# One rounding moved behind a product in block 1, and six matmuls moved forward in the last down projection

## The chip, the cores and the metric

The kernel runs on one NeuronCore of a Trainium2 chip. The metric is the device time of one execution in microseconds (us). The kernel before took 323.59 us, the median of three runs (323.27, 323.59, 323.6).

## What is computed

The input x has 128 batch rows, 32 channels and 512 positions. The reference does this:

```python
y = irfft(rfft(u, 2L) * rfft(K, 2L))[..., :L] + u * D     # one long convolution per channel, K from the parameters
y = y * mask                                              # positions below a length
gate = fp8(y / s) @ gate_w.T ;  up = fp8(y / s) @ up_w.T  # 512 -> 1376
hidden = silu(gate) * up
out = x + fp8(hidden / s) @ down_w.T                      # 1376 -> 512
```

`fp8` clips to 448, rounds to float8_e4m3 and gives the value back as a wide number. The kernel builds that rounding from ordinary operations: a magnitude (ACT), a sum with the magnitude (DVE), a difference that leaves the rounded value in bf16 (DVE), and a clip (DVE).

## The kernel before, in words

The 32 channels are worked in 8 blocks of 4 (`NBLK` = 8, g counts them), so that a block has 512 tokens (4 channels x 128 batch rows). For a block g there are three kinds of work:

- **convolution** of each channel h with its Toeplitz tile (PE, L528 into `y_ps`), masked by DVE (`mask_y`, L882), scaled and its magnitude taken by ACT (`scale_y`, L378 and L379; `magnitude_y`, L386 and L389), and rounded by DVE (`sum_y` L890, `round_y` L901, `clip_y` L908) into `yq`;
- **gate and up products**: the 1376 hidden features are cut into 11 chunks (`CH` = 11) of 128, the last of 96. A chunk takes 4 matmuls into `gate_ps` and 4 into `up_ps` (L604, each double buffered). ACT makes `sil` (L415), DVE the product `hv` (`product`, L917). Chunks go in pairs (`PAIRS` = 6, the last is one chunk): ACT takes the magnitude `hc` of a pair (`abs_prod`, L397), DVE makes `ht` (`rounded_sum`, L925), rounds into `hq` (`rounded`, L934) and clips `hq` in place (`clip`, L942);
- **down projection** of the block: four row tiles t of 128 tokens, each 11 matmuls over the chunks k (`down_part`, L542), brought out by ACT (`down_scaled`, L405).

Every engine runs its own list in program order, written by hand in `slots`. Slot c of block g holds chunk c of block g, a part of the down projection of block g-1 and a part of the convolution of blocks g+1 and g+2. So when block g begins, the rounding of the last pairs of block g-1 is still to be done. On DVE that is `left_over` (L952): pairs 3, 4 and 5 of the block before, spread over slots 0, 1 and 2. It has two orders, chosen by `behind`. `behind` is true for the last block alone (L977). The ACT list of block 1 has, behind `sil` of slot 1, the magnitude of the left-over pair 5, then two magnitudes and two scalings of block 2's y, and only then `sil` of slot 2 (L408 ff.). The last block has no y work beside it.

What PE waits for: chunk n needs the products up to n-2 and `sil` up to n-2, because the banks are double buffered; the down projection of a block needs `hq_ready` for the pair of its chunk, which `clip` counts (chunks 8 and 9 are pair 4, chunk 10 is pair 5). In block 1 chunks 6 to 9 of row tile 0 are in slot 3, chunk 10 is in slot 4.

The last down projection (L645 to L660, the profile's L655) follows the last block and has no other work beside it. Row tile t has its own bank; tile 3 is computed as columns 0 to 383 and then columns 384 to 511. DVE adds the residual x to each finished tile (`residual`, L949) and SP stores it (L282); the last store ends the kernel.

Of the kernel before, what the change touches and what calls it, by code (L numbers as in the profile page):

```python
# [28 lines left out]
P = 128  # L29
# [4 lines left out]
NBLK = C // HB  # L34
TOK = HB * B
LB = L // P
CH = -(-I // P)
# [32 lines left out]
def width(c):  # L70
    return P if c < CH - 1 else TAIL
# [7 lines left out]
def adaln_ffn_kernel(nc, xT, xn, params, scales, unit, stepped, wg_d, wu_d, wd_d, out):  # L79
# [4 lines left out]
    with ExitStack() as ctx:  # L84
# [124 lines left out]
        def last_bank(t, cols):  # L209

            return gate_ps[0] if cols.start else (down_ps[0], down_ps[1], y_ps[0], y_ps[1])[t]
# [247 lines left out]
        def _(pe):  # L459
# [183 lines left out]

            full = slice(0, L)
            for t, chunks, cols in ((0, range(6), full), (1, range(6), full), (0, range(6, 8), full), (1, range(6, 8), full),  # L645
                                    (2, range(6), full), (0, range(8, CH), full), (1, range(8, CH), full),
                                    (2, range(6, CH), full), (3, range(CH), slice(0, 3 * P)),
                                    (3, range(CH), slice(3 * P, L))):
                for k in chunks:
                    w = width(k)  # L650
                    if t == 0:
                        pe.wait_ge(hq_ready, PAIRS * (NBLK - 1) + k // 2 + 1)
                    if k == 0:
                        pe.wait_ge(out_done, EMPTY + HB * (NBLK - 2) + t + 1)
                    mm = nc.tensor.matmul(last_bank(t, cols)[:, cols], hq[1][0:w, k, t * P:(t + 1) * P],  # L655
                                          wd[0:w, k, cols], start=(k == 0), stop=(k == CH - 1))
                    if k == CH - 1:
                        mm.then_inc(down_ready, 1)
# [3 lines left out]
        def _(dve):  # L662
# [214 lines left out]
            def mask_y(g, h):  # L877
                m = HB * g + h
                q = h % 2
                at_least(dve, y_ready, m + 1)  # L880
                at_least(dve, yscaled, m - 1)
                v.tensor_tensor(ym[q][:], y_ps[q][:], mask[:].rearrange("p k b -> p (k b)"),  # L882
                                ALU.mult).then_inc(ym_done, 1)

            def sum_y(g, h):

                m = HB * g + h
                q = h % 2
                at_least(dve, yscaled, m + 1)
                v.scalar_tensor_tensor(yt[q][:], yc[q][:], FLOOR, yv[q][:], ALU.max, ALU.add).then_inc(yt_done, 1)  # L890
# [4 lines left out]
            def round_y(g, par, h):  # L895

                m = HB * g + h
                q = h % 2
                at_least(dve, yt_done, m + 1)
                at_least(dve, up_ready, CH * (g - 1))  # L900
                v.scalar_tensor_tensor(yq_of(par, h), yc[q][:].rearrange("p v (k b) -> p (v k) b", k=LB), FLOOR,  # L901
                                       yt[q][:].rearrange("p v (k b) -> p (v k) b", k=LB), ALU.max, ALU.subtract,
                                       reverse1=True).then_inc(yr_done, 1)

            def clip_y(g, par, h):

                at_least(dve, yr_done, HB * g + h + 1)
                v.tensor_scalar(yq_of(par, h), yq_of(par, h), TOP, -TOP, ALU.min, ALU.max).then_inc(yq_ready, 1)  # L908

            def product(n, m, par, c):  # L910

                b, w = (par + c) % 2, width(c)
                at_least(dve, silu_done, n + 1)
                at_least(dve, up_ready, n + 1)
                if c % 2 == 0:
                    at_least(dve, t_done, m - 2)
                v.scalar_tensor_tensor(hv[c // 2 % 3][0:w, c % 2], up_ps[b][0:w, :], fac[0:w, S_UP:S_UP + 1],  # L917
                                       sil[b][0:w, :], ALU.mult, ALU.mult).then_inc(prod_done, 1)

            def rounded_sum(m, e):  # L920

                w, k = pair_rows(e)
                at_least(dve, abs_ready, m + 1)
                at_least(dve, hr_done, m - 1)
                v.scalar_tensor_tensor(ht[e % 2][0:w, 0:k], hc[e % 2][0:w, 0:k], FLOOR, hv[e % 3][0:w, 0:k],  # L925
                                       ALU.max, ALU.add).then_inc(t_done, 1)

            def rounded(m, g, par, e):

                w, k = pair_rows(e)  # L930
                at_least(dve, t_done, m + 1)
                if e == 0:
                    at_least(dve, down_ready, READ + HB * (g - 1))
                v.scalar_tensor_tensor(hq[par][0:w, 2 * e:2 * e + k, :], hc[e % 2][0:w, 0:k], FLOOR,  # L934
                                       ht[e % 2][0:w, 0:k], ALU.max, ALU.subtract, reverse1=True).then_inc(hr_done, 1)

            def clip(m, par, e):

                w, k = pair_rows(e)
                at_least(dve, hr_done, m + 1)  # L940
                part = hq[par][0:w, 2 * e:2 * e + k, :]
                v.tensor_scalar(part, part, TOP, -TOP, ALU.min, ALU.max).then_inc(hq_ready, 1)  # L942
# [31 lines left out]

            def slots(g, par, ahead, before, plan):
                first = before is None
                behind = g == NBLK - 1  # L977
                for c in range(CH):
                    n = CH * g + c
                    m = PAIRS * g + c // 2  # L980
                    if first and c == 3:
                        rounded(m - 1, g, par, 0)
                    product(n, m, par, c)
                    if c == 0 and g - 1 in SUM_BEHIND:
                        clip(PAIRS * g - 4, 1 - par, PAIRS - 4)
                        rounded_sum(PAIRS * g - 2, PAIRS - 2)
                    if c == CH - 1 and c in plan:
                        rounded(PAIRS * g + plan[c], g, par, plan[c])
                    if c % 2 == 0 and 0 < c < CH - 1:
                        rounded_sum(m - 1, c // 2 - 1)  # L990
                    if first and c == 1:
                        round_y(1, 1, 0)
                        clip_y(1, 1, 0)
                    elif ahead and c in MASK_PLAN:
                        mask_y(g + 1, MASK_PLAN[c])
                    if c < 3 and not first:
                        left_over(g, par, c, before, behind)
                    if c in plan and c < 9 and not (first and c == 3):
                        rounded(PAIRS * g + plan[c], g, par, plan[c])
                    if ahead and c in SUM_PLAN and not (first and c == 2):  # L1000
                        sum_y(g + 1, SUM_PLAN[c])
                    if c - 1 in plan:
                        clip(PAIRS * g + plan[c - 1], par, plan[c - 1])
                    if ahead and c in ROUND_PLAN and not (first and c == 4):
                        round_y(g + 1, 1 - par, ROUND_PLAN[c])
                        clip_y(g + 1, 1 - par, ROUND_PLAN[c])
                    if c == 9 and c in plan:
                        rounded(PAIRS * g + plan[c], g, par, plan[c])
                    if c == CH - 1:
                        if ahead == 2:  # L1010
                            mask_y(g + 2, 0)
                        if g not in SUM_BEHIND:
                            if PAIRS - 3 not in plan.values():
                                clip(PAIRS * g + PAIRS - 4, par, PAIRS - 4)
                            rounded_sum(m - 1, PAIRS - 2)
# [38 lines left out]
            sum_y(1, 0)  # L1054
            dve.wait_ge(k_ready, 2 * len(K_GROUPS))
            slots(0, 0, 2, None, H_BEHIND)
            for stored_k in k_stored:
                dve.wait_ge(stored_k, 16)
            slots(1, 1, 2, H_BEHIND, H_BEHIND)
            slots(2, 0, 2, H_BEHIND, H_EVEN)  # L1060
            for g in range(3, NBLK - 2):
                slots(g, g % 2, 2, H_EVEN, H_EVEN)
# [28 lines left out]
SUM_BEHIND = (0, NBLK - 2)  # L1091
# [63 lines left out]
```

## Time and profile before

| what | value |
|---|---|
| median of three runs | 323.59 us |
| the profiled execution's own time | 324.86 us |
| its span | 323.2 us |
| PE, matmuls busy | 310.3 us (96%) |
| DVE busy | 303.1 us (94%) |
| ACT busy | 206.5 us (64%) |
| granted TensorE clock over the span | 1.0 |

The span is the time from the first to the last instruction of the profiled execution; the execution's own time is 1.66 us longer. A matmul's record is longer than its share of a stream of matmuls: neighbours overlap. The same holds for DVE's and ACT's records, so steps are read from one start to the next. PEld is the weight load of a matmul.

### The profile page before, as it was taken

The numbers are of one execution on the slowest core, as the hardware profiler recorded it, in microseconds if no ns is written. First come the engines' busy times: TensorE is split into PE (matmuls) and PEld (weight loads), VectorE is DVE, ScalarE is ACT, GpSimd is POOL, SyncE is SP. The second block draws the span as 40 slices with busy tenths as digits, with TensorE's granted clock in tenths as the row PEclk, the third lists the DMA queues.
The fourth block names the chain that finished last, engine by engine and source line by source line (L and its number), as shares of the span: only waits on it lengthen the run. The fifth ranks groups of instructions, "written<-read, shape, count | busy, mean of one in ns | idle before, by whom it ended". The sixth has DMA issues, their size and how long they took to land.

```text
span 323.2 us, 4716 instructions
## 1 busy us (share of the span) xinstructions
PE 310.3 (96%) x1591; PEld 161.8 (50%) x1591; DVE 303.1 (94%) x460; ACT 206.5 (64%) x318; POOL 13.7 (4%) x25
## 2 busy tenths in 40 slices
PE   1979999999999999999999999999999999999996
PEld 1456655545455454555455454555545554444443
DVE  6969999999999999999989999899998999999894
ACT  4938788278765868376863958366864859545550
POOL 3031000000001000010001000010000000010010
PEclk9999999999999999999999999999999999999999
DMA  6869999500001690067401690046600770070028
GB/s 201 170 174 218 240 292 363 220 1 2 0 0 13 128 357 26 1 117 243 159 0 16 126 360 19 0 80 202 239 0 0 132 261 0 3 130 0 0 26 235
DMA packets 14015, 38.42 MB, mean 119 GB/s; under 512 B 1470, under 2 KB 6558, under 8 KB 11052
## 3 DMA queue, kind: packets, MB, share of 16 engines
q1 hardware_dynamic: 8412, 26.61, 23.9%
q0 software_dynamic: 5584, 11.57, 20.5%
q8 instruction: 10, 0.16, 0.2%
q14 instruction: 9, 0.07, 0.1%
HBM read 33.93 MB, written 15.81 MB: 154 GB/s over the span
## 4 chain that ended last, share of the span: by engine, by line
PE 77%; DVE 15%; issue 3%; DMA 3%; ACT 2%; DVEq 0%; SPq 0%
PE gate_ps L604 20%; PE up_ps L604 20%; PE down_ps L542 17%; PE y_ps L528 15%; DVE hv L917 3%; DVE yq L901 2%; DVE ht L925 2%; DVE yt L890 2%; DVE hq L934 2%; PE down_ps L558 2%; PE y_ps L558 1%; DMA toep<-kpad_scratch 1%; DVE ym L882 1%; PE y_ps L655 1%; DMA kpad_scratch<-hq 1%
## 5 line engine op out<-in xcount | busy, mean ns | idle before, releaser
L415 ACT ACTIVATE sil<-gate_ps,fac 128x512 f32<-128x512 f32 (+1 forms) x88 | 59.8, 681 | 71.4 <-PE gate_ps L604 70.5
L604 PE MATMUL gate_ps<-yq,wg 128*128 128x512 bf16 (+2 forms) x372 | 89.5, 363 | 0.5 <-DVE hv L917 0.3
L604 PE MATMUL up_ps<-yq,wu 128*128 128x512 bf16 (+2 forms) x372 | 89.5, 363 | 0.0
L528 PE MATMUL y_ps<-xt,toep 128*128 128x512 f32 (+1 forms) x248 | 78.1, 434 | 0.0
L917 DVE SCALAR_TENSOR_TENSOR hv<-up_ps,fac,sil 128x512 f32<-128x512 f32 (+1 forms) x88 | 65.5, 744 | 6.9 <-ACT sil L415 3.5
L542 PE MATMUL down_ps<-wd,hq 128*128 128x512 bf16 (+1 forms) x264 | 67.9, 379 | 0.0
L397 ACT ACTIVATE hc<-hv 128x1024 f32<-128x1024 f32 (+1 forms) x48 | 47.0, 980 | 17.1 <-DVE hq L934 16.7
L604 PEld LDWEIGHTS gate_ps<-yq,wg 128*128 128x128 bf16 x372 | 36.0, 100 | 41.0 <-issue 2.2
L528 PEld LDWEIGHTS y_ps<-xt,toep 128*128 128x128 f32 x248 | 45.8, 190 | 20.0 <-issue 2.4
L604 PEld LDWEIGHTS up_ps<-yq,wu 128*128 128x128 bf16 x372 | 36.3, 100 | 38.3
L925 DVE SCALAR_TENSOR_TENSOR ht<-hc,hv 128x1024 f32<-128x1024 f32 (+1 forms) x48 | 54.2, 1129 | 0.9 <-ACT hc L397 0.9
L934 DVE SCALAR_TENSOR_TENSOR hq<-hc,ht 128x1024 bf16<-128x1024 f32 (+1 forms) x48 | 53.9, 1126 | 0.3
L542 PEld LDWEIGHTS down_ps<-wd,hq 128*128 128x128 bf16 (+1 forms) x264 | 25.8, 98 | 32.7 <-issue 12.0
L901 DVE SCALAR_TENSOR_TENSOR yq<-yc,yt 128x1024 bf16<-128x1024 f32 x32 | 39.0, 1219 | 0.4
L890 DVE SCALAR_TENSOR_TENSOR yt<-yc,yv 128x1024 f32<-128x1024 f32 x31 | 37.7, 1216 | 0.0
L386 ACT ACTIVATE yc<-ym,fac 128x512 f32<-128x512 f32 x32 | 22.9, 715 | 3.4 <-DVE yq L901 3.0
L378 ACT ACTIVATE yv<-ym,fac 128x512 f32<-128x512 f32 x31 | 22.1, 712 | 3.4 <-DVE ym L882 3.4
L389 ACT ACTIVATE yc<-ym,fac 128x512 f32<-128x512 f32 x32 | 22.8, 713 | 0.0
L379 ACT ACTIVATE yv<-ym,fac 128x512 f32<-128x512 f32 x31 | 22.0, 709 | 0.0
L882 DVE TENSOR_TENSOR ym<-y_ps,mask 128x512 f32<-128x512 f32 x31 | 21.1, 680 | 0.2 <-PE y_ps L528 0.2
L942 DVE TENSOR_SCALAR hq<-hq 128x1024 bf16<-128x1024 bf16 (+1 forms) x48 | 18.5, 396 | 0.3
L405 ACT ACTIVATE res<-down_ps,fac 128x512 f32<-128x512 f32 x26 | 17.6, 677 | 1.0 <-PE down_ps L542 1.0
(163 smaller groups left out, 133.8 us busy)
## 6 DMA issues: line engine op xcount, KB each, us to landing
xt<-in_xT SPq DMA_DIRECT2D x8, 1024.0 KB, 7.8
out<-in_x SPq DMA_DIRECT2D x7, 1024.0 KB, 5.7
out<-res POOLq DMA_DIRECT2D x7, 1024.0 KB, 7.7
toep<-kpad_scratch SPq DMA_DIRECT2D x6, 1024.0 KB, 10.1
toep<-kpad_scratch SPq DMA_DIRECT2D x8, 256.0 KB, 5.1
wd<-in_down POOLq DMA_DIRECT2D x1, 1280.0 KB, 21.9
xt<-in_x SPq DMA_DIRECT2D x1, 1024.0 KB, 7.4
out<-xt SPq DMA_DIRECT2D x3, 256.0 KB, 3.2
```

What stands on the lines that cost most here:

```text
L386: gate = nc.scalar.activation(yc[q][:, 0, :], ym[q][:], ACT.Abs, scale=fac[:, R_GATE:R_GATE + 1])
L397: nc.scalar.activation(hc[e % 2][0:w, 0:k], hv[e % 3][0:w, 0:k], ACT.Abs, scale=UP20).then_inc(abs_ready, 1)
L415: nc.scalar.activation(sil[b][0:w, :], gate_ps[b][0:w, :], ACT.Silu, scale=fac[0:w, S_GATE:S_GATE + 1]).then_inc(silu_done, 1)
L528: last = nc.tensor.matmul(y_ps[h % 2][:, d * P:L], toep[par][:, h, d * P:(d + 1) * P], xt[par][:, h, 0:L - d * P], start=(d == 0), stop=(d ...
L542: mm = nc.tensor.matmul(down_ps[t % 2][:], hq[par][0:w, k, t * P:(t + 1) * P], wd[0:w, k, :], start=(k == 0), stop=(k == CH - 1))
L604: mm = nc.tensor.matmul(ps[b][0:w, cols], wt[:, k, c * P:c * P + w], yq[par][:, version, k, cols], start=(k == 0), stop=(k == LB - 1))
L882: v.tensor_tensor(ym[q][:], y_ps[q][:], mask[:].rearrange("p k b -> p (k b)"), ALU.mult).then_inc(ym_done, 1)
L890: v.scalar_tensor_tensor(yt[q][:], yc[q][:], FLOOR, yv[q][:], ALU.max, ALU.add).then_inc(yt_done, 1)
L901: v.scalar_tensor_tensor(yq_of(par, h), yc[q][:].rearrange("p v (k b) -> p (v k) b", k=LB), FLOOR, yt[q][:].rearrange("p v (k b) -> p (v k ...
L917: v.scalar_tensor_tensor(hv[c // 2 % 3][0:w, c % 2], up_ps[b][0:w, :], fac[0:w, S_UP:S_UP + 1], sil[b][0:w, :], ALU.mult, ALU.mult).then_i ...
L925: v.scalar_tensor_tensor(ht[e % 2][0:w, 0:k], hc[e % 2][0:w, 0:k], FLOOR, hv[e % 3][0:w, 0:k], ALU.max, ALU.add).then_inc(t_done, 1)
L934: v.scalar_tensor_tensor(hq[par][0:w, 2 * e:2 * e + k, :], hc[e % 2][0:w, 0:k], FLOOR, ht[e % 2][0:w, 0:k], ALU.max, ALU.subtract, reverse ...
```

## The change

Two edits. On DVE, `left_over` takes its `behind` order in block 1 as well as in the last block (block 1 is the one whose block before, 0, is in `SUM_BEHIND` = (0, 6)). With it, in block 1, the rounding of block 0's pair 4 stands behind block 1's second product instead of ahead of it, and the clip of pair 4 with the rounding and the clip of pair 5 stands in slot 2 behind the third product and the first sum of block 1, instead of in slot 1. In the last down projection the chunks 0 to 5 of row tile 3 (columns 0 to 383) are issued ahead of chunks 8 to 10 of row tile 0.

```diff
-                                    (2, range(6), full), (0, range(8, CH), full), (1, range(8, CH), full),
-                                    (2, range(6, CH), full), (3, range(CH), slice(0, 3 * P)),
+                                    (2, range(6), full), (3, range(6), slice(0, 3 * P)),
+                                    (0, range(8, CH), full), (1, range(8, CH), full),
+                                    (2, range(6, CH), full), (3, range(6, CH), slice(0, 3 * P)),
                                     (3, range(CH), slice(3 * P, L))):
...
             def slots(g, par, ahead, before, plan):
                 first = before is None
-                behind = g == NBLK - 1
+                behind = g - 1 in SUM_BEHIND
```

DVE's order in slots 0 to 2 of block 1, where s, r and c are sum, rounding and clip of a pair and a stroke marks block 1's own pair:

```
before: product 0, c2, s4, mask, r3, r4 | product 1, c3, c4, s5, r5, c5 | product 2, s0', sum_y
after:  product 0, c2, s4, mask, r3     | product 1, c3, r4, s5         | product 2, s0', c4, r5, c5, sum_y
```

## Rows read from the trace of the kernel before

**Rows 1.** Stretches: length, busy us of PE, PEld, DVE, ACT, POOL, clock, DMA, GB/s.
```profile
75.20:85.60 10.40, 10.36 (x47) 4.87 (x45) 10.37 (x14) 7.21 (x11) 0.00 (x0) 1.00 0.01 2
...
100.00:285.00 185.00, 185.00 (x870) 95.77 (x868) 178.44 (x227) 124.25 (x188) 5.21 (x6) 1.00 0.39 109
```

**Rows 2.** The chain of waits, 72 to 86 us: start, us, what.
```profile
72.44 1.02 PE gate_ps L604 x4
...
75.62 0.86 PE down_ps L542 x4
...
85.56 0.09 issue
```

**Rows 3.** DVE in order of time, 69 to 85 us: start, us, engine, line, operation.
```profile
69.29 2.35 DVE L934 SCALAR_TENSOR_TENSOR hq<-hc,ht 128x1024 bf16<-128x1024 f32 x2
71.56 0.74 DVE L917 SCALAR_TENSOR_TENSOR hv<-up_ps,fac,sil 128x512 f32<-128x512 f32 x1
72.22 0.75 DVE L942 TENSOR_SCALAR hq<-hq 128x1024 bf16<-128x1024 bf16 x2
72.89 0.68 DVE L925 SCALAR_TENSOR_TENSOR ht<-hc,hv 96x512 f32<-96x512 f32 x1
73.60 0.69 DVE L934 SCALAR_TENSOR_TENSOR hq<-hc,ht 96x512 bf16<-96x512 f32 x1
74.32 0.29 DVE L942 TENSOR_SCALAR hq<-hq 96x512 bf16<-96x512 bf16 x1
74.53 0.74 DVE L917 SCALAR_TENSOR_TENSOR hv<-up_ps,fac,sil 128x512 f32<-128x512 f32 x1
75.23 1.23 DVE L925 SCALAR_TENSOR_TENSOR ht<-hc,hv 128x1024 f32<-128x1024 f32 x1
76.37 1.22 DVE L890 SCALAR_TENSOR_TENSOR yt<-yc,yv 128x1024 f32<-128x1024 f32 x1
...
83.16 1.22 DVE L901 SCALAR_TENSOR_TENSOR yq<-yc,yt 128x1024 bf16<-128x1024 f32 x1
84.41 0.43 DVE L908 TENSOR_SCALAR yq<-yq 128x1024 bf16<-128x1024 bf16 x1
84.75 0.75 DVE L917 SCALAR_TENSOR_TENSOR hv<-up_ps,fac,sil 128x512 f32<-128x512 f32 x1
```

**Rows 4.** ACT in order of time, 70 to 75 us, idle time before in brackets.
```profile
70.59 0.63 ACT L397 ACTIVATE hc<-hv 96x512 f32<-96x512 f32 x1 [1.61 <-DVE hq L934]
...
73.58 0.67 ACT L415 ACTIVATE sil<-gate_ps,fac 128x512 f32<-128x512 f32 x1
74.15 1.04 ACT L397 ACTIVATE hc<-hv 128x1024 f32<-128x1024 f32 x1
```

**Rows 5.** PE in order of time, slot 2 of block 1.
```profile
71.16 1.03 PE L542 MATMUL down_ps<-wd,hq 128*128 128x512 bf16 x4
```

**Rows 6.** The last block's slots 1 and 2, in order of time.
```profile
290.65 1.06 ACT L397 ACTIVATE hc<-hv 128x1024 f32<-128x1024 f32 x1 [0.93 <-DVE hq L934]
...
291.74 1.23 DVE L925 SCALAR_TENSOR_TENSOR ht<-hc,hv 128x1024 f32<-128x1024 f32 x1
```

**Rows 7.** Busy time by stretch, 18 to 22 us, columns as in rows 1.
```profile
18.00:22.00 4.00, 2.87 (x14) 2.42 (x15) 1.59 (x5) 0.91 (x2) 0.63 (x1) 1.00 0.52 186
```

**Rows 8.** The last down projection in order of time.
```profile
315.17 0.59 PE L655 MATMUL down_ps<-wd,hq 128*128 128x512 bf16 x2
315.73 0.29 DVE L942 TENSOR_SCALAR hq<-hq 96x512 bf16<-96x512 bf16 x1
316.08 1.04 PE L655 MATMUL down_ps<-wd,hq 96*128 96x512 bf16 x4 [0.32 <-DVE hq L942]
...
320.03 0.62 DVE L949 SCALAR_TENSOR_TENSOR xt<-y_ps,fac,xt 128x384 f32<-128x384 f32 x1 [1.04 <-PE y_ps L655]
```

**Rows 9.** The chain of waits at the end.
```profile
317.12 2.89 PE y_ps L655 x16
```

**Rows 10.** Busy time by stretch at the end, columns as in rows 1.
```profile
321.00:321.50 0.50, 0.00 (x0) 0.00 (x0) 0.00 (x1) 0.00 (x0) 0.00 (x0) 1.00 0.55 209
```

## The prediction, written before the run

> **What bounds the kernel now.** I read the chain of waits first, then the busy time by stretch, then the engines in order of time around both edits. The windows say where which of the two sets the pace: from 100 to 285 us PE is busy 185.00 of 185 us [rows 1], so nothing that PE loses before 100 us is ever won back; whatever delay it has at that point arrives whole at the end. From 75.2 to 85.6 us both are full: PE 10.36 and DVE 10.37 of 10.40 us [rows 1]. The chain tells how the two meet there: it leaves DVE for PE at 72.44, where the matmuls of block 1's chunk 3 begin behind product 1, and has one more crack at 85.56, an issue piece of 0.09 us ahead of chunk 7 [rows 2], whose matmuls start at 85.64. Chunk 7 needs product 5, which starts at 84.75 and takes 0.75 us [rows 3], so it is done at 85.50: chunk 7 too starts as soon as DVE lets it. Between the two DVE has no gap. The reader is to see that DVE's list from 69.29 to 85.50 is one unbroken chain that ends in a PE start, and that PE cannot catch up behind it.
>
> In the tail PE waits between the second matmul of 315.17 and the matmul of 316.08, for the clip of the last pair, 315.73 to 316.02 [rows 8].
>
> **Part 1, what it takes away.** The two roundings of 69.29 take 2.27 us to the start of product 1 (71.56 - 69.29), 1.13 each [rows 3]. With one of them gone from in front, product 1 starts at 70.42 instead of 71.56 and ends near 71.2. Chunk 3 then finds its bank free, and PE is held only by its own stream. Its four matmuls before were issued at one per 0.216 us (0.86 for four [rows 2]); from the down matmuls ahead of chunk 3, which start at 71.16 [rows 5], that gives 72.02 instead of 72.44. So 0.42 us of a PE stall goes.
>
> **Part 1, what it adds.** DVE's new order is product 1, clip 3, rounding 4, sum 5, product 2. From 70.42: product 0.66 (71.56 to 72.22), clip 0.33 (two in 0.67), rounding 1.13, sum 0.71 (72.89 to 73.60) [rows 3]; DVE would be ready for product 2 at 73.25. But product 2 needs `sil` of slot 2, and that is ACT's: ACT starts the magnitude of pair 5 at 70.59, released by rounding 3, which does not move, and works through without a bracket until `sil` of 73.58, done at 74.25 [rows 4]. Nothing in that row of seven ACT operations waits for anything that the change moves earlier. So DVE idles from 73.25 to 74.28 (74.25 and 0.03 for the semaphore). Product 2 takes 0.67 to 74.95. Next is sum 0 of block 1, which needs the magnitude that ACT runs from 74.15 to 75.19 [rows 4]: it starts at 75.22, against 75.23 before [rows 3]. DVE has idled 1.03 + 0.27 = 1.30 us, and sum 0 is where it was.
>
> Before, that time was filled: clip 4, rounding 5 and clip 5 stood ahead of product 2. Now they stand behind sum 0. Their steps are 0.33, 0.72 (73.60 to 74.32) and 0.21 (74.32 to 74.53), together 1.26 us [rows 3]. So `sum_y` starts at 77.62 instead of 76.37, 1.25 us late, and everything behind it on DVE with it.
>
> At one place a rule bears on these steps. A rounding whose clip follows at once takes longer to the next start than one with another operation behind it: 83.16 to 84.41 is 1.25 us, against 1.13 for the same size [rows 3]. The Trainium skill ("VectorE: DVE Perf Modes", The DRAIN you can't avoid) says of Vector operations in a row that "the semaphore costs nothing extra here". The row speaks otherwise, and clip 5 stands right behind rounding 5 in both orders; by the rule the three moved steps would be about 0.1 us shorter and the sum of part 1 by as much less.
>
> **Who waits for the late work.** Two things, and the later one counts.
> (a) The down matmuls of slot 3 need clip 4 at their third matmul. Before, they start at 75.62 [rows 2], so the third at 76.05; without the stall of chunk 3 at 75.63. Clip 4 now starts at 76.36, takes 0.41 (the second of the two of 72.22 ends at 72.97, 0.42 behind its start at 72.55 [rows 3]), and PE follows a clip's end 0.06 us later (316.02 to 316.08 [rows 8]): 76.83. PE stalls 1.20 us and is 0.78 us later than before (76.83 - 76.05). Pair 5's clip ends near 77.7, ahead of its matmul in slot 4, near 80.
> (b) Chunk 7 needs product 5. DVE has no gap between 75.23 and 84.75, so product 5 is the full 1.25 us late and chunk 7 starts at 85.64 + 1.25 = 86.89. By (a) alone it would be ready at 85.56 + 0.78 = 86.34; so DVE sets it.
> Nothing else is late by more: products 3 and 4, 1.25 us later, still end 0.7 us or more ahead of chunks 5 and 6, which move by 0.78. Queued on ACT behind its waits for DVE are magnitudes and `sil` of slots 4 to 6, which move by as much as their producers. Behind chunk 7 both engines are shifted alike, so no new wait comes of it, and POOL's and SP's transfers in this stretch move with the blocks (the DMA share there is 0.01 [rows 1]).
>
> Part 1 therefore costs **1.25 us**. The gain of 0.42 us isn't to be subtracted: it lies ahead of the point where DVE sets the start. Even if DVE's delay were nil, chunk 7 would start at 85.64 as before, so the best that part 1 can do is 0.0 to 0.1 us. The bounds: 0 us below, and above 1.5 us, if also a dependent step (0.12) and one more semaphore are lost.
>
> **Part 2.** PE is free of waits to 315.17 in both kernels. Before, it runs two matmuls there (0.43 us, to 315.60) and stands until 316.08: 0.48 us [rows 8]. Six matmuls of 384 columns take less than full ones. The 16 matmuls of 2.89 us are 5 of 512 columns at 0.216 and 11 of 384 [rows 9], so one of 384 is (2.89 - 1.08)/11 = 0.165 us, six are 0.99 us. After, tile 0's chunk 8 starts at 316.16, chunk 10 at 316.59, 0.57 us behind the end of the last clip (316.02 [rows 8]): no wait is left, and from 315.17 on the same matmuls run without a gap. The end of tile 3 comes 0.48 us earlier. Tiles 0, 1 and 2 come 0.99 - 0.48 = 0.51 us later; DVE stands 1.04 us ahead of tile 3's residual at 320.03 [rows 8]; the residual of tile 2 comes 0.51 us later and this one 0.48 us earlier, so 0.05 us of that is left and DVE isn't in the way. No bank is added: tile 3's was emptied by ACT before 312 us.
>
> Not all of it reaches the end. Between 321.0 and 321.5 us the DMA engines are busy 0.55 of the time [rows 10], with the stores of tile 2 behind and those of tile 3 ahead. Three stores of 256 KB come 0.51 us later and the last two 0.48 us earlier, so they draw together by 1 us and that thin piece is filled. The bounds are 0.48 us (no crowding) and 0.2 us (45% of half a us is empty, and nothing else is won). I take 0.42, near the upper one: the last store, 64 KB, has only the 192 KB of tile 3 right ahead of it.
>
> **Sum.** 1.25 - 0.42 = +0.83 us. The profiled execution would go from 324.86 to 325.69 us, its span from 323.2 to 324.0. Its own time lies 1.27 us above the median shown, which is the execution and not the work; set on the median, 323.59 + 0.83 = **324.4 us**.
>
> **The rivals.**
> *ACT isn't in the way* (not slower). It decides at one point: if `sil` of slot 2 is done before 73.3 us, DVE doesn't idle, and the same work in another order takes the same time. For it: the last block has this order already, and there sum 0 starts at 291.74, and ACT's magnitude for it, done at 291.71, came after ACT had been waiting 0.93 us for DVE [rows 6]. Against it: that ACT has no y work in its list, while in block 1 four y activations fill ACT's time between the magnitude of 70.59 and `sil` of 73.58, without a gap [rows 4]. Price of part 1 zero: 323.59 - 0.42 = 323.2 us. 12%.
> *DVE catches up before chunk 7*, so that only PE's stall in slot 3 counts: 0.78 - 0.42 = +0.36, 323.95 us. It needs 0.5 us of air in DVE's list between 75.2 and 85.5, where the row has 0.03 [rows 1]. 10%.
> *The tail gains nothing*, since the stores crowd each other or the last residual waits for the one ahead: +1.25, 324.85 us. For it: the 0.05 us of room on DVE [rows 8], and a window of which only 45% is empty [rows 10]. 12%.
> *The clock falls in the new stalls* of 1.20 us and 0.55 us: if some 6 us of matmuls took twice their time that is 3 us more, 327.4 us. Against it: between 18 and 22 us PE was busy 2.87 of 4.00 us at granted clock 1.00 [rows 7], that is the 2.4 GHz level. [...] 2%.
>
> **Chances.** The forecast itself, 324.1 to 324.7 us, has 64%. A measurement of this kernel tells about 0.2%, 0.65 us, from no change; slower by more is above 324.24. The forecast lies above that by a little, so of its 64% I give 55 to slower and 9 to the same; the tail rival and the clock make slower 0.69; the second rival and most of the first make the same 0.28, and 0.03 is left for faster, where the first rival and a full tail gain meet. The range for 8 in 10: 323.6 to 324.9 us, which leaves out most of the first rival and the clock.
>
> **What would show it.** In the profile after: a gap on DVE ahead of block 1's product 2 with ACT's `sil` as releaser, about 1 us; a small one ahead of sum 0; the chain running over ACT from 70.6 to 75.2 us; PE waiting about 1.2 us for the clip in slot 3 and about half a us ahead of chunk 7; no wait ahead of chunk 3; from there the same rows 1.25 us later. In the tail no PE wait ahead of tile 0's chunk 10. The prediction is wrong if product 2 starts without a gap, if chunk 7 starts within 0.5 us of 85.64, or if the last block's end differs from its distance to the tail's start.

## The result and the profile after

| | before | after |
|---|---|---|
| median | 323.37 us (6 runs, 323.15 to 323.6) | 324.53 us (6 runs, 324.34 to 324.89) |
| ratio | | 1.0036, 95% interval 1.0023 to 1.0049 |
| the profiled execution's own time, and its span | 324.86, 323.2 us | 324.38, 322.7 us |

The change made the kernel slower by 1.16 us (0.36%; the interval is 0.74 to 1.58 us). The forecast was 324.4 us and slower.

The two spans say the opposite: after is 0.5 us shorter. They can't be compared as they are, because the profiled execution of before began late. This is the first convolution matmul in the order of time on PE, before and then after:

```profile
19.14 0.92 PE L617 MATMUL y_ps<-xt,toep 128*128 128x256 f32 x4 [2.00 <-DMA toep<-kpad_scratch]
```
```profile
17.61 0.92 PE L617 MATMUL y_ps<-xt,toep 128*128 128x256 f32 x4 [0.41 <-DMA toep<-kpad_scratch]
```

In the execution before, the first Toeplitz load landed late and everything behind it is 1.53 us late, in code that the change does not touch. All eleven experiments below start this matmul between 17.37 and 17.78 us. The profiled execution before lies 1.49 us above its median (324.86 against 323.37), about what this load explains. I compare stretches from here on, each measured from the start of rounding 3 in block 1 (69.29 us before, 67.77 after), which no edit moves.

A bracket in these rows is the idle time ahead of an operation and what ended it. It counts from the end of the record before, and a record reaches past the point at which the next one could start: four matmuls have a record of 1.02 or 1.03 us and take 0.86 us to the next start. So from start to start a PE wait is 0.16 or 0.17 us longer than its bracket, and a wait shorter than that has no bracket.

The changed stretch on DVE, after, in order of time (lines are one higher than before: L918 is `product`, L926 the sum, L935 the rounding, L943 the clip, L891 `sum_y`):

```profile
67.77 1.21 DVE L935 SCALAR_TENSOR_TENSOR hq<-hc,ht 128x1024 bf16<-128x1024 f32 x1
68.90 0.74 DVE L918 SCALAR_TENSOR_TENSOR hv<-up_ps,fac,sil 128x512 f32<-128x512 f32 x1
69.56 0.41 DVE L943 TENSOR_SCALAR hq<-hq 128x1024 bf16<-128x1024 bf16 x1
69.89 1.22 DVE L935 SCALAR_TENSOR_TENSOR hq<-hc,ht 128x1024 bf16<-128x1024 f32 x1
71.03 0.68 DVE L926 SCALAR_TENSOR_TENSOR ht<-hc,hv 96x512 f32<-96x512 f32 x1
72.76 0.75 DVE L918 SCALAR_TENSOR_TENSOR hv<-up_ps,fac,sil 128x512 f32<-128x512 f32 x1 [1.05 <-ACT sil L415]
73.71 1.23 DVE L926 SCALAR_TENSOR_TENSOR ht<-hc,hv 128x1024 f32<-128x1024 f32 x1 [0.20 <-ACT hc L397]
74.85 0.42 DVE L943 TENSOR_SCALAR hq<-hq 128x1024 bf16<-128x1024 bf16 x1
75.18 0.68 DVE L935 SCALAR_TENSOR_TENSOR hq<-hc,ht 96x512 bf16<-96x512 f32 x1
75.90 0.29 DVE L943 TENSOR_SCALAR hq<-hq 96x512 bf16<-96x512 bf16 x1
76.11 1.21 DVE L891 SCALAR_TENSOR_TENSOR yt<-yc,yv 128x1024 f32<-128x1024 f32 x1
...
84.49 0.74 DVE L918 SCALAR_TENSOR_TENSOR hv<-up_ps,fac,sil 128x512 f32<-128x512 f32 x1
```

Against [rows 3]: two brackets have appeared, 1.05 us ahead of product 2 for ACT's `sil` and 0.20 us ahead of sum 0 for ACT's magnitude. The sum starts 5.94 us behind rounding 3 in both kernels (75.23 - 69.29, 73.71 - 67.77). Three operations that stood ahead of it stand behind it, and `sum_y` comes at 8.34 us instead of 7.08, product 5 at 16.72 instead of 15.46: 1.26 us.

What PE makes of it, after, its waits (the first of each group) in order of time:

```profile
75.32 0.60 PE L542 MATMUL down_ps<-wd,hq 128*128 128x512 bf16 x2 [1.21 <-DVE hq L943]
...
85.38 1.02 PE L604 MATMUL gate_ps<-yq,wg 128*128 128x512 bf16 x4 [0.37 <-DVE hv L918]
```

PE stands 1.21 us in slot 3 for clip 4 and 0.37 us ahead of chunk 7, by the brackets; from start to start it is 1.37 and 0.54 us. The chain of waits after shows where the time sits. Before, it left DVE for PE ahead of chunk 3 and stayed on PE up to chunk 7 [rows 2]. Now it passes through ACT's row from 69.07 on, then DVE, and it goes back to DVE ahead of chunk 7:

```profile
69.07 0.10 ACT hc L397
...
72.15 0.57 ACT sil L415
72.73 0.96 ACT hc L397
...
73.71 1.23 DVE ht L926
74.93 0.35 DVE hq L943
...
75.32 0.60 PE down_ps L542 x2
...
84.49 0.76 DVE hv L918
85.24 0.14 issue
85.38 1.02 PE gate_ps L604 x4
```

The tail after, in order of time, and the half microsecond with the clock times of [rows 10]:

```profile
313.61 2.43 PE L656 MATMUL y_ps<-wd,hq 128*128 128x512 bf16 x12
315.46 0.29 DVE L943 TENSOR_SCALAR hq<-hq 96x512 bf16<-96x512 bf16 x1
315.88 1.46 PE L656 MATMUL down_ps<-wd,hq 128*128 128x512 bf16 x6
...
319.90 0.35 DVE L950 SCALAR_TENSOR_TENSOR xt<-gate_ps,fac,xt 128x128 f32<-128x128 f32 x1
```
```profile
321.00:321.50 0.50, 0.00 (x0) 0.00 (x0) 0.00 (x0) 0.00 (x0) 0.00 (x0) 1.00 1.03 382
```

PE no longer waits for the last clip, which ends at 315.75. The six matmuls of 315.88 are chunks 8 to 10 of row tiles 0 and 1; the one that needs this clip, tile 0's chunk 10, is the third, near 316.31, held by nothing but the stream. The last residual ends 0.48 us nearer to the tail's first matmul. But behind it the DMA engines are full where they had been thin. The last residual ends at 321.00 before and at 320.25 after. The half microsecond right behind it had a DMA share of 0.55 before; after, the half microsecond from 320.25 has 0.99, and the row shown, 0.75 us behind the residual, has 1.03. The end of the span follows the last residual by 2.45 us instead of 2.2.

One thing does run beside the last down projection: block 6's accumulating store of 1 MB, which POOL issues at 312.25 us before and at 311.99 after. It takes 7.7 us to land in both, so it still moves data while the first stores of the last block do.

All kernels of this study, by four stretches of their profiled executions (the last one to 0.05 us, since a span is given to 0.1):

| kernel | rounding 3 to chunk 7 | rounding 3 to the tail's first matmul | from there to the end of the last residual | from there to the end | median us |
|---|---|---|---|---|---|
| before | 16.35 | 241.13 | 10.58 | 2.2 | 323.37 |
| after | 17.61 | 242.38 | 10.10 | 2.45 | 324.53 |
| e1 block 1 only | 17.61 | 242.38 | 10.58 | 2.15 | 324.55 |
| e2 tail only | 16.35 | 241.12 | 10.09 | 2.67 | 323.20 |
| e3 rounding only | 16.36 | 241.71 | 10.58 | 2.18 | 323.34 |
| e4 ACT later | 16.38 | 241.16 | 10.09 | 2.50 | 323.31 |
| e5 tail, three | 16.35 | 241.12 | 10.10 | 2.30 | 322.97 |
| e6 before, fewer stores | 16.35 | 241.13 | 10.57 | 2.17 | 323.16 |
| e7 tail, fewer stores | 16.37 | 241.14 | 10.09 | 2.22 | 322.72 |
| e8 best | 15.85 | 240.62 | 10.09 | 2.59 | 322.63 |
| e9 clip later | 16.10 | 240.87 | 10.59 | 2.17 | 323.21 |
| e10 clip and rounding | 16.02 | 241.04 | 10.58 | 2.13 | 323.17 |
| e11 best, three | 15.85 | 240.62 | 10.10 | 2.57 | 322.79 |

The first of these stretches is called the distance below. The kernel before, run beside the experiments, had medians of 323.27 us (e1 to e8) and 323.31 us (e9 to e11).

### The profile page after: what moved, and what is told of

The parts are those of the page before. It is cut to its first block, busy times and chain, and to the rows that moved or that the text cites. A ratio compares the mean times of both kernels' runs of the same rounds, so it can differ in the third digit from the quotient of the medians.

```text
span 322.7 us, 4716 instructions
## 1 busy us (share of the span) xinstructions
PE 310.6 (96%) x1591; PEld 162.0 (50%) x1591; DVE 303.3 (94%) x460; ACT 206.6 (64%) x318; POOL 13.7 (4%) x25
## 4 chain that ended last, share of the span: by engine, by line
PE 75%; DVE 16%; issue 3%; ACT 3%; DMA 2%; DVEq 0%; ACTq 0%; SPq 0%
PE gate_ps L604 19%; PE up_ps L604 19%; PE down_ps L542 16%; PE y_ps L528 14%; DVE hv L918 3%; DVE yq L902 3%; DVE ht L926 2%; DVE ym L883 2%; DVE yt L891 2%; PE down_ps L558 2%; PE y_ps L558 1%; PE down_ps L656 1%; DVE hq L935 1%; PE y_ps L656 1%; DMA toep<-kpad_scratch 1%
## 5 line engine op out<-in xcount | busy, mean ns | idle before, releaser
L918 DVE SCALAR_TENSOR_TENSOR hv<-up_ps,fac,sil 128x512 f32<-128x512 f32 (+1 forms) x88 | 65.5, 745 | 7.9 <-ACT sil L415 4.6
L926 DVE SCALAR_TENSOR_TENSOR ht<-hc,hv 128x1024 f32<-128x1024 f32 (+1 forms) x48 | 54.2, 1128 | 1.1 <-ACT hc L397 1.1
L935 DVE SCALAR_TENSOR_TENSOR hq<-hc,ht 128x1024 bf16<-128x1024 f32 (+1 forms) x48 | 54.0, 1126 | 0.2
L891 DVE SCALAR_TENSOR_TENSOR yt<-yc,yv 128x1024 f32<-128x1024 f32 x31 | 37.7, 1216 | 0.0
L943 DVE TENSOR_SCALAR hq<-hq 128x1024 bf16<-128x1024 bf16 (+1 forms) x48 | 18.6, 397 | 0.3
## 6 DMA issues: line engine op xcount, KB each, us to landing
toep<-kpad_scratch SPq DMA_DIRECT2D x6, 1024.0 KB, 10.2
```

## The experiments

**The two edits apart.** e1 is the kernel before with `behind = g - 1 in SUM_BEHIND`; e2 is the kernel before with the tail's new order.

> The change's first edit alone: block 1 takes the other order of the left-over pairs, the last down projection is as in the kernel before. Theory (DVE idles behind ACT in block 1, and what it puts off there arrives at chunk 7): about 1.25 us slower than the kernel before, 324.6 us; in the profile a DVE gap of 1.0 us ahead of block 1's product 2 and 0.2 ahead of sum 0, PE waits 1.2 us for the clip in slot 3, and the distance from the start of the first rounding of pair 3 to chunk 7's first matmul is 17.6 us against 16.35 before. Rival (most of the loss is made elsewhere, by a start that varies or by the tail): under 0.6 us slower.

Measured: 324.55 us, ratio 1.0038 (1.0024 to 1.0052), 1.28 us slower. The gaps on DVE are 1.05 and 0.20 us, PE's wait 1.21 us, the distance 17.61 us. The theory's numbers are met one by one, and the rival is out: this edit alone makes the whole slowdown, within what a run tells.

> The change's second edit alone: six matmuls of row tile 3 ahead of those that need the last clips. Theory (PE's stall of 0.48 us goes, and the stores give back half of it because they start closer together): 0.2 to 0.3 us faster than before, 323.1 us; from the last DVE operation to the end of the span 2.4 to 2.5 us against 2.2 before. Rival (the stores' 0.25 us was chance of one execution): the full 0.42 to 0.48 us, 322.9 us, and 2.2 us behind the last DVE operation.

Measured: 323.20 us against 323.27, ratio 0.9997 (0.9988 to 1.0006), no difference. The last residual is 0.49 us earlier and the end follows it by 2.67 us instead of 2.2, more than either theory said: in this profile the stores give back 0.47 of 0.49 us. The times alone say less. Their interval reaches from 0.39 us faster to 0.19 slower, so it holds the theory's 0.2 to 0.3 us and leaves out the rival's 0.42 to 0.48.

**Is it ACT's row?** e4 is the changed kernel with ACT's two scalings taken from slot 1 to slot 2, behind `sil` and the magnitude, in each of the blocks 1 to 6:

```diff
+                    if ahead and c == 2 and not first:
+                        scale_y(g + 1, 1)
                     if ahead and c in MAGNITUDE_PLAN ...
...
-                    if ahead and c in SCALE_PLAN and not (first and SCALE_PLAN[c][1] == 0):
+                    if ahead and c in SCALE_PLAN and not (first and SCALE_PLAN[c][1] == 0) and (first or c != 1):
```

> The changed kernel, with one thing moved on ACT: in blocks 1 to 6 the two scalings of the next block's channel 1 go from slot 1 to slot 2, behind sil and the pair's magnitude, so that sil of slot 2 is done 1.2 us earlier. Theory (ACT's list is what DVE waits for in block 1): the DVE gaps of 1.05 and 0.20 us go, PE's 1.2 us wait for the clip shrinks to under 0.1 us, chunk 7 starts at the distance of the kernel before; about 1.2 us faster than the changed kernel, 323.2 us. Rival (the late clips and roundings cost by their place alone, for PE's sake): the gap goes but PE still waits 0.5 us or more in slot 3 and the time stays at 324 us or above.

Measured: 323.31 us, ratio to the kernel before 0.9999 (0.9990 to 1.0008); that is 1.2 us faster than the changed kernel. DVE's order is that of the changed kernel, and its gap ahead of product 2 is gone. DVE of e4 in order of time (L928 the sum, L920 the product, L945 the clip):

```profile
71.21 0.68 DVE L928 SCALAR_TENSOR_TENSOR ht<-hc,hv 96x512 f32<-96x512 f32 x1
71.81 0.74 DVE L920 SCALAR_TENSOR_TENSOR hv<-up_ps,fac,sil 128x512 f32<-128x512 f32 x1
72.66 1.22 DVE L928 SCALAR_TENSOR_TENSOR ht<-hc,hv 128x1024 f32<-128x1024 f32 x1
73.80 0.42 DVE L945 TENSOR_SCALAR hq<-hq 128x1024 bf16<-128x1024 bf16 x1
```

Product 2 follows sum 5 by 0.60 us, without a bracket, and the distance to chunk 7 is 16.38. Of the second wait something is left: sum 0 starts 0.85 us behind product 2, where a product takes 0.66 to the next start if nothing holds it (68.90 to 69.56 in the profile after). PE's stop in slot 3 is down to 0.15 us from start to start (chunk 4 starts 6.77 us behind rounding 3, against 6.62 in e3, which has no stop); under 0.1 was expected. So the loss was not the late place of the clip but the idle time behind ACT that came with it.

**What the removed stall is worth.** In e3 the rounding alone goes behind product 1:

```diff
+                if g == 1:
+                    if c == 0:
+                        rounded(last - 2, g - 1, 1 - par, PAIRS - 3)
+                    if c == 1:
+                        clip(last - 2, 1 - par, PAIRS - 3)
+                        rounded(last - 1, g - 1, 1 - par, PAIRS - 2)
+                        rounded_sum(last, PAIRS - 1)
...
```

The rest of the edit keeps clip 4, rounding 5 and clip 5 behind sum 5, ahead of product 2.

> Against the kernel before, only pair 4's rounding goes behind product 1 in block 1; the clip of pair 4 and the rounding and clip of pair 5 stay ahead of product 2; the tail is as before. Theory (DVE's unbroken list sets chunk 7's start, so the PE stall of 0.42 us ahead of chunk 3 is worth nothing, and the put-off work is what costs): no stall ahead of chunk 3, no DVE gap above 0.1 us, chunk 7 at most 0.1 us earlier than before; 323.3 us, within 0.2 us of the kernel before. Rival A (the removed stall is worth its 0.42 us): 322.9 us. Rival B (moving the rounding itself costs, whatever stands behind it): 0.5 us slower or more.

Measured: 323.34 us, ratio 1.0 (0.9991 to 1.0009). The stall ahead of chunk 3 is gone, and the wait ahead of chunk 7 has grown in its place, as PE of e3 shows:

```profile
83.89 1.02 PE L604 MATMUL gate_ps<-yq,wg 128*128 128x512 bf16 x4 [0.50 <-DVE hv L917]
```

From start to start the wait is 0.67 us (82.36 + 0.86 = 83.22, to 83.89), where it was 0.25 in the kernel before: 0.42 more, the whole of the stall that went. The distance is 16.36 us, that of before. Both rivals are out: the stall is worth nothing by itself, and the moved rounding costs nothing by itself. The profiled execution of e3 has one more thing in it, under the last heading.

e9 moves block 1's clip of pair 0 behind product 5, e10 makes both moves:

```diff
-                    if c - 1 in plan:
+                    if c - 1 in plan and not (g == 1 and c == 4):
                         clip(PAIRS * g + plan[c - 1], par, plan[c - 1])
+                    if g == 1 and c == 5:
+                        clip(PAIRS * g, par, 0)
```

> The kernel before with one thing moved: block 1's clip of pair 0 (0.33 us) behind product 5 instead of ahead of it. Pair 4's rounding stays ahead of product 1. Theory (chunk 7 starts at the later of DVE's product 5 and PE's own stream, and PE's stream still holds the 0.42 us stall of chunk 3): product 5 is 0.33 us earlier, chunk 7 only 0.08 to 0.1 us, distance from rounding 3 to chunk 7 16.26 us, 323.2 us. Rival (DVE alone sets the time): distance 16.02, 322.95 us.

> Both small moves together, tail and ACT as before: pair 4's rounding behind product 1 with the other left-over work still ahead of product 2, and the clip of pair 0 behind product 5. Theory (each alone is worth 0.0 and 0.1 us because the other limit holds; together the later of two earlier limits counts): distance 16.02 us, 0.33 us less than before, 322.95 us. Rival (they are worth no more together than apart): distance 16.25, 323.2 us.

Measured: e9 323.21 us, ratio 1.0002 (0.9993 to 1.0011); e10 323.17 us, ratio 0.9993 (0.9984 to 1.0002). The times tell neither from no change. The distances tell more: 16.10 and 16.02 us. In e9 product 5 starts 0.33 us earlier (15.13 us behind rounding 3) and PE's stream carries straight into chunk 7, so 16.10 is where PE's own limit lies with the stall of chunk 3 in it. Expected was 16.26. In e10 that limit has moved and DVE's 16.02 counts, as expected to the digit. So chunk 7 does start at the later of two limits, DVE's and PE's; only PE's lay 0.16 us lower than I had read it. That the 0.25 and 0.33 us arrive in the times was not shown.

**Where the tail's gain goes.** e5 moves three matmuls instead of six (`(3, range(3), ...)` and `(3, range(3, CH), ...)`). e6 and e7 leave out the stores of row tiles 0 and 1 (`if t < 2: continue` in SP's loop), e6 on the kernel before, e7 on the new order of the tail.

> The kernel before with the tail's edit halved: three matmuls of row tile 3 go forward instead of six. They take 0.495 us, just PE's stall of 0.48, so row tiles 0 to 2 end where they did before and the last two stores still start 0.48 us earlier. Theory A (what is given back comes of the early stores being 0.5 us late): 2.2 us from the last DVE operation to the end, time 0.4 to 0.48 us faster, 322.85 us. Theory B (the last stores are held by the data of the stores ahead, whenever these start): 2.4 to 2.7 us behind the last DVE operation as with six, and 0.1 to 0.25 us faster, 323.1 us.

> The kernel before without the stores of the last block's row tiles 0 and 1 (left out), all else the same. A base for the next run. Theory (the last store waits for other stores' data by a little): behind the last DVE operation 1.9 to 2.2 us, 0 to 0.3 us faster than before.

> The second edit alone, and the stores of row tiles 0 and 1 left out. Theory (stores that draw together cost the 0.25 to 0.5 us): with half of the data gone the time behind the last DVE operation is the same as in the run before, within 0.1 us, and the kernel is 0.45 us faster than that one. Rival (the end costs more for another reason, such as SP's list): it stays 0.25 us or more above that of the run before.

Measured: e6 323.16 us (ratio 0.9995, 0.9986 to 1.0004) and 2.17 us behind the last residual; e7 322.72 us (0.9982, 0.9973 to 0.9991) and 2.22 us. With the two stores gone, the new order is worth 0.44 us, nearly the whole 0.48 that PE wins, against 0.07 with them. Each of these times is known to some 0.3 us, so the profiles have to carry the reading, and they do. The last store, 64 KB, takes from its issue to its landing:

| kernels | last store, us |
|---|---|
| old order, all stores (before, e1, e3, e9, e10) | 1.7 in each |
| six matmuls moved, all stores (after, e2, e4, e8) | 2.0, 2.2, 2.1, 2.1 |
| three moved, all stores (e5, e11) | 1.9, 2.2 |
| two stores left out, old and new order (e6, e7) | 1.7, 1.7 |

SP isn't what is late: its last issue ends 0.48 us behind the last residual in the kernel before, 0.50 after, 0.51 in e2 and 0.52 in e7. So the last stores wait for the data of the stores ahead of them. How large a part block 6's accumulating store has in this is open, since no run leaves it out.

e5 has 322.97 us, ratio 0.9986 (0.9978 to 0.9995), and 2.30 us: between its two theories and nearer to neither; the 0.30 us of the times stand between theory B's 0.25 and theory A's 0.4.

**A version that beats both kernels.** e8 joins e3's order, e9's clip, e4's ACT and the tail's edit; e11 is e8 with three matmuls moved in the tail.

> A version built on what was found: pair 4's rounding behind product 1 with the other left-over work ahead of product 2, block 1's clip of pair 0 (0.33 us) behind product 5 instead of ahead of it, ACT's two scalings of slot 1 behind sil of slot 2, and the tail's edit. Theory (DVE's list sets chunk 7, and PE could start it 0.5 us earlier than before): the distance from rounding 3 to chunk 7 falls from 16.35 to 15.9 us, the tail gives 0.1, together 0.5 to 0.6 us faster than before, 322.8 us. Rival (chunk 7 isn't DVE's): distance at 16.3, 323.2 us.

> The best version so far with three matmuls moved forward in the tail instead of six. Theory (the stores crowd less): 2.3 us behind the last DVE operation instead of 2.6, 0.2 us faster than that version, 322.4 us, 0.8 to 0.9 us faster than the kernel before. Rival (the end is chance): 322.6 us.

Measured: e8 322.63 us, ratio 0.9973 (0.9962 to 0.9984), 0.64 us faster than the kernel before; the distance is 15.85 us, and no bracket is left on PE between 66 and 90 us. From start to start chunk 7 still waits 0.16 us: it starts 0.89 us behind product 5, as in the kernel before (84.75 to 85.64), so DVE sets it here too. e11 has 322.79 us, ratio 0.9985 (0.9976 to 0.9993), 0.52 us faster than the kernel before and on another chip than e8, and 2.57 us behind the last residual where 2.3 was expected. Its theory failed: in this version three moved matmuls are no better than six. The 2.3 of e5 may have been the chance of one execution; its time, 0.30 us below the kernel before, was not explained.

## Why the prediction was right

The total was +0.83 us, measured +1.16 (0.74 to 1.58). The forecast of 324.4 us lies only 0.13 from the measured 324.53, and part of that is luck: it was built on a median before of 323.59 us, which came out at 323.37 in six runs. The 0.22 us of the start hid most of the 0.33 by which the change itself was sized too small. Of the signs named as proof of an error one needs care: chunk 7 starts at 85.38 us, within 0.5 us of 85.64, but only because the profile before is late by its first load; from rounding 3 it is 17.61 us against 16.35. Step by step:

- **DVE idles behind ACT.** Foretold 1.03 and 0.27 us. The brackets are 1.05 and 0.20, but the forecast was reckoned from start to start, and so measured the waits are 1.13 (71.03 + 0.60 to 72.76) and 0.29 (72.76 + 0.66 to 73.71). The 0.10 us more of the first is the time that sum 5 was given too much, which the next point explains. Product 2 starts 4.99 us behind rounding 3 and sum 0 5.94, foretold 4.99 and 5.93. In e4 the first wait is gone with ACT's order changed and 0.19 us is left of the second. This is the step that decided the sign.
- **The three operations put off, 1.26 us.** 75.18 to 76.11 and the clip ahead of them (74.85 to 75.18) are 1.26 us. The step of rounding 5 with its clip right behind is 0.72 (75.18 to 75.90), as taken. Sum 5 takes 0.60 to the next start where something else follows (e4) and 0.71 where its own rounding does [rows 3]. A dependent follower costs 0.11 us, against what I quoted from the Trainium skill ("VectorE: DVE Perf Modes", The DRAIN you can't avoid). The measurement decides.
- **The later of the two at chunk 7.** DVE's delay set it: 17.61 - 16.35 = 1.26 us, foretold 1.25. The matmul that needs clip 4 starts 7.55 us behind rounding 3, foretold 7.54. That its bracket of 1.21 us meets the foretold wait of 1.20 is chance: from start to start PE waits 1.37 us, because without the wait it would have been 0.16 us earlier than I had it. That the 0.42 us of the stall is not to be subtracted was the second choice that mattered, and e3 shows it.
- **PE's own limit at chunk 7 was read too late.** I took 85.56 from the chain's issue piece of 0.09 us. PE of the kernel before in order of time says otherwise:

```profile
83.67 1.03 PE L604 MATMUL up_ps<-yq,wu 128*128 128x512 bf16 x4
84.53 1.03 PE L542 MATMUL down_ps<-wd,hq 128*128 128x512 bf16 x4
85.64 0.59 PE L604 MATMUL gate_ps<-yq,wg 128*128 128x512 bf16 x2
```

  Four matmuls take 0.86 us to the next start (83.67 to 84.53), so chunk 7 could have started at 85.39, and the wait is 0.25 us. A piece of the chain begins where the record before it ends, not where the operation starts. e9 has that limit, at 16.10 and not 16.26. It changed nothing in the sum; but part 1's best case was 0.25 us, not 0.1, for a version in which DVE is faster. For the same reason PE was 0.97 us late at chunk 4 (8.00 against 7.03 us behind rounding 3) and not 0.78. The room of "0.7 us or more" ahead of chunk 6 was 0.57 by the forecast's own terms (83.02 to 83.59); measured it is 0.74 (81.51 to 82.25), so nothing waited there.
- **The tail, the term mis-sized.** PE's 0.48 us came as foretold. I took 0.42 of it for the end; the stores gave back 0.25 us in the profile after, 0.47 in e2, and e2's times keep 0.07, below my lower bound of 0.2. The changed kernel against e1 says the same: 324.53 and 324.55 us, with and without the tail's edit. The reason that I gave for the lower bound, the thin half microsecond, was the right one: it is full now. The choice of the upper bound was wrong, because I asked what lies right ahead of the last store and not how much data all five have between them. With 0.07 in place of 0.42 the sum is 1.18 us.
- **The rivals.** *ACT isn't in the way* is refuted by the two gaps and by e1, *DVE catches up* by the distance, *the clock falls* by the profile after: between 75 and 76 and between 84 and 86 us, around stalls of 1.21 and 0.37 us, the granted clock is 1.00, the 2.4 GHz level. The "6 us of matmuls" of that rival's price came from no row. *The tail gains nothing* was the nearest to the truth in its part and got 12%; its 324.85 us is 0.3 above the measured time.

## What to carry to other kernels

Work that stands ahead of an operation that waits for another engine may be free only there: before it is moved behind, ask what time the operation could really start, and by whose list, not only what the moved work delays. A stall that is removed ahead of a point where another engine sets the start is worth nothing, and the worth of two such moves is that of the later limit. When a forecast of a wait is compared with a profile, both must be counted the same way, from start to start. For a last matmul group, count the bytes of all the stores that must still drain before calling an earlier end a gain, and compare two profiles from an event that neither edit touches, not by their spans.

## What the runs showed that was not expected

The profiled execution of e3 loses 0.57 us between chunk 7 and the tail, in one place: PE of e3 in block 2, in order of time.

```profile
123.24 1.12 PE L528 MATMUL y_ps<-xt,toep 128*128 128x512 f32 x2 [0.32 <-DMA toep<-kpad_scratch]
```

Its chain reaches back over two transfers:

```profile
101.71 8.71 DMA out<-res
...
112.08 10.94 DMA toep<-kpad_scratch
```

Block 0's accumulating store has to land before SP goes on to the Toeplitz load of block 4. It took 8.7 us here against 7.8 in the kernel before. In the kernel before, the load is issued at 112.9 us, takes 10.2 us and lands at 123.1, 1.4 us ahead of the matmul at 124.52. Over the kernels here the same load took 9.3 to 11.1 us. So this chain has little room, and two slow transfers in one execution use it up. e10, whose accumulating store took 8.7 us too, loses 0.24 us in the same stretch; it also reaches rounding 3 50.63 us behind its first convolution matmul, where the kernel before takes 50.15. The profiled execution of e9 loses nothing there. How often the other executions do is open, and so is why e9 and e10 show less in their times than in their distances.
